# Cross-attention with the values stationary in four column tiles, and the probabilities' sums taken by VectorE and ones

## The chip, the cores and the metric

One core of a Trainium2 chip runs the whole program. The metric is the device time of one execution in microseconds (us); lower is better. Three executions of the kernel before took 1486.96, 1487.69 and 1585.24 us, with 1487.69 us as their median.

## What is computed

The input is x of shape (16, 64, 512) and a context of shape (16, 1601, 256), all in float32. A cross-attention reads the context, a causal self-attention and a mixture of experts follow. The change lies in the cross-attention. Cut to what matters here:

```
q  = ln(x @ Wq + bq)                     # 16 heads of 32
k, v of the first 1585 context rows;  k2, v2 of the last 16 rows ("second" attention)
ctx  = softmax(q k^T / sqrt(32)) v       # over 1585 rows
ctx += softmax(q k2^T / sqrt(32)) v2     # over 16 rows
x = x + ctx @ Wo + bo
```

For each of the 16 batches and 16 heads, 64 queries are weighed over 1585 and over 16 rows. Both softmaxes are normalised after the weighted sum, so the kernel needs, for each query and head, the sum of the exponentials of each attention.

## The kernel before, in words

**Work and its pieces.** The context of a batch is cut into 13 chunks of 128 rows (`CH` = 13); the 13th chunk of two batches shares one tile (49 rows each), and the 16 rows of the second attention lie in that same tile. So two batches, one turn of the outer loop `i`, make 25 projections (`PROJ`) and 26 units of attention (`UNITS`). The units stand in groups (`GROUP`, line 41): five groups of two units and one of three for each batch, 12 groups a turn, 8 turns.

**One group on each engine.** The order is written out by hand in `steps` of each engine.

- TensorE, for each chunk: `keys` (six matmuls of 512 columns into `K_BANK`), `values` (six more into `V_BANK`), `turn` (four transposes of the normalised keys of the group before). Then `weighted` for this group's units and `scores` for the next group's units.
- VectorE, in `chunks`: for each chunk `k_bias` (line 1133, reads PSUM and adds the bias), `k_reduce` (line 1139, sums the squares) and `k_norm` (lines 120, 122, 124 on 16 numbers a row, then line 1148 over 512). The norm of a chunk stands behind the bias of the next one. `queries` (line 1156) copies the next batch's queries in groups 5 and 11; `second_keys` (line 1165) follows groups 1 and 2.
- GpSimd (POOL): `square` (line 1088, the squares of `kc`) and `y_low` (line 1081, the low part of a context chunk).
- ScalarE (ACT): `exps` (line 1004, one of 128x1024 for a unit, into `probs`), `v_evac` (990), `k_evac` (976), `y_high` (963) and `seed` (113 and 115: the start value for the norm).
- SyncE issues the loads.

Every engine works through its own list in order. `keys` of a chunk waits for `k_bias` of the chunk before (semaphore kb), `turn` for `k_norm` of its chunk (km), `weighted` for the exponentials (ex).

**The step that is changed.** In `weighted` (lines 1283 to 1299) the probabilities of a head (128 rows of context by 64 queries) are the stationary operand, and the head's values with a column of ones behind them (`VW1` = 33 columns) move through. Even and odd heads go to PSUM partitions 0 to 63 and 64 to 127, that is two column tiles of 64. The 33rd column of the result is the sum of the probabilities.

```
last = pe.matmul(psum[j * SQ:(j + 1) * SQ, V_BANK if n else O_BANK, p * VW1:(p + 1) * VW1],
                 probs[:, buf(u), place(h) * SQ:(place(h) + 1) * SQ], v, ...)
```

There are 16 such calls for a unit, 32 for the last unit of a batch (which also does the second attention). The trace holds two records for each call with float32 operands. After the last unit ScalarE copies both results to `o_sb` (`o_evac`, 128x264 each), VectorE inverts the sums (line 1209, 16 numbers a row), POOL multiplies and adds (`normalise`, lines 871 and 873, three operations of 128x256), TensorE transposes the result (`turn_ctx`, line 1305), and ScalarE copies it to `ctxT` (`ctx_evac`).

Of the kernel before, what the change touches and what calls it, by code (L numbers as in the profile page):

```python
# [36 lines left out]
VW1 = HD + 1  # L37
# [116 lines left out]
def prepare(nc, io, g, psum):  # L154
    with ExitStack() as ctx:
# [10 lines left out]
        bq = g.o_sb[:].rearrange("p a q n -> p (a q n)")[:, 0:D]  # L166
# [43 lines left out]
        with nc.Block() as block:  # L210
# [102 lines left out]
            def _(pool):  # L313
# [10 lines left out]
                nc.gpsimd.memset(g.v[:], 1.0)  # L324
                nc.gpsimd.memset(g.ctx[:], 0.0)
# [4 lines left out]
                for n, col in enumerate((6, 7, 10, 11)):  # L330
                    nc.gpsimd.tensor_tensor(g.v_last[:, n // 2, n % 2, :, HD], g.v_last[:, n // 2, n % 2, :, HD],
                                            g.cols[:, col:col + 1].to_broadcast([P, H]), ALU.add)
# [413 lines left out]
def cross_attention(nc, io, g, psum):  # L746
# [3 lines left out]
    with ExitStack() as ctx:  # L750
# [4 lines left out]
        kc, o_sb, rinv, od = g.kc, g.o_sb, g.rinv, g.od  # L755
# [8 lines left out]
        probs = sb("probs", [P, 3, H * SQ])  # L764
        select = sb("select", [2, 3, P])
# [45 lines left out]
        def last_unit(u):  # L811

            return u - UNITS + CH if u == TAIL else u - CH if u == UNITS - 1 else u - 2 if column(u) >= 2 else u - 3

# [52 lines left out]

        def normalise(b, wait, engine):

            for n, dst in enumerate((g.ctx, od)):  # L870
                engine.tensor_tensor(dst[:], o_sb[:, n, :, 0:HD], spread(rinv[:, n], HD), ALU.mult).then_inc(s["onp"], 1)
            wait.wait_ge(s["onp"], b * 2 + 2)
            engine.tensor_tensor(g.ctx[:], g.ctx[:], od[:], ALU.add).then_inc(s["on"], 1)

        with nc.Block() as block:
# [69 lines left out]
            def _(act):  # L945
# [5 lines left out]
                act.sem_inc(s["ce"], 1)  # L951
# [55 lines left out]
                def o_evac(b, i, u):  # L1007

                    act.wait_ge(s["pv"], unit(i, u))
                    act.wait_ge(s["on"], b + 1)  # L1010
                    nc.scalar.copy(o_sb[:, 1], psum[:, V_BANK, 0:PAIRS * VW1].rearrange("p (q n) -> p q n", n=VW1))
                    nc.scalar.copy(o_sb[:, 0], psum[:, O_BANK, 0:PAIRS * VW1].rearrange("p (q n) -> p q n", n=VW1))\
                        .then_inc(s["oe"], 1)

                def ctx_evac(b):

                    act.wait_ge(s["ct"], b + 1)
                    nc.scalar.copy(g.ctxT[:, :, :, bass.ds(b * SQ, SQ)],
                                   psum[:, TR_BANK, 0:2 * P].rearrange("p (g j q) -> p g j q", g=2, j=2)).then_inc(s["ce"], 1)
# [22 lines left out]
                def steps(i, room, guarded):  # L1042
                    for group in range(GR):
# [4 lines left out]
                        if group in (1, 7):  # L1048
                            ctx_evac(i * 2 + group // 6)
# [20 lines left out]
            def _(pool):  # L1070
                pool.sem_inc(s["ksq"], PROJ)
                pool.sem_inc(s["ylo"], PROJ + EARLY)
                pool.sem_inc(s["on"], 1)
# [51 lines left out]
            def _(dve):  # L1125
                for stage in ("kb", "krd", "kn1", "kn2", "krs", "km"):
                    dve.sem_inc(s[stage], PROJ)

# [39 lines left out]
                def chunks(i, ns):  # L1168

                    for j, n in enumerate(ns):  # L1170
                        k_bias(i, n)
                        if j:
                            k_norm(i, ns[j - 1])
                        k_reduce(i, n)
                    if ns:
                        k_norm(i, ns[-1])

                def first(guarded):
# [3 lines left out]
                    chunks(0, projections(2, GR))  # L1182
# [20 lines left out]
                def steps(i, room, guarded):  # L1203
                    for group in range(1, GR + 1 if room else GR):
                        if group in (5, 11) and (group == 5 or room):
                            queries(i * 2 + (1 if group == 5 else 2), i, TAIL if group == 5 else UNITS - 1, guarded)
                        if group in (6, 12):
                            dve.wait_ge(s["oe"], i * 2 + (group // 6 + 1))
                            nc.vector.reciprocal(rinv[:], o_sb[:, :, :, HD]).then_inc(s["rc"], 1)
# [1337 lines left out]
```

## Time and profile before

| | us |
|---|---|
| median of three executions | 1487.69 |
| span of the profiled execution, first to last instruction | 1487.2 |
| TensorE matmuls busy | 1399.9 |
| TensorE weight loads busy | 1181.9 |
| VectorE busy | 860.5 |
| ScalarE busy | 778.8 |
| GpSimd busy | 500.8 |

The cross-attention fills the span from about 70 to 1180 us; what comes before prepares the weights and queries, what comes behind it is self-attention and the experts. Times in the trace's views count from the span's start. A timeline row gives start, length, engine, line, operation, result and operands, shapes, and the count of merged instructions; in brackets stands how long the engine sat idle before it, and which instruction ended that.

### The profile page before, as it was taken

To read this page: it belongs to the slowest core of one execution; us is meant where nothing else is said; L and a number is where in the kernel's file an instruction comes from. 1 tells how busy PE (TensorE), PEld (TensorE's weight loads), DVE (VectorE), ACT (ScalarE), POOL (GpSimd) and SP (SyncE) were. 2 spreads that over 40 slices of the span, in tenths; PEclk is the share of its full clock that TensorE was granted. 3 is DMA by queue.
4 is the path that set the end of the run, shared out by engine and by line. 5 is a ranking of instruction groups with operands and counts; after the bars stand their busy time and mean duration, and the time that the engine had idled before them with its cause. 6 is when DMAs were issued, how large, how long until landed. Compare 5 with 4: busy or idle time off the path is not lost. (4 is left out here: it accounts for less than half of the span.)

```text
span 1487.2 us, 41615 instructions
## 1 busy us (share of the span) xinstructions
PE 1399.9 (94%) x15754; PEld 1181.9 (79%) x15754; DVE 860.5 (58%) x2005; ACT 778.8 (52%) x1560; POOL 500.8 (34%) x550
## 2 busy tenths in 40 slices
PE   6789999999999999999999999999999899984796
PEld 3378888888888888888888888888878677764696
DVE  7756555655655565556456555655555356655764
ACT  2345555655555565555555555555555433333653
POOL 3333333333333333333333333333323121111455
PEclk9999999999999999999999999999999999995999
DMA  7042110210111121102101101211010100004886
GB/s 253 19 158 77 31 30 16 91 31 16 62 46 30 30 78 30 30 16 92 30 16 62 48 28 30 78 30 31 17 74 2 60 3 30 30 30 178 220 182 140
DMA packets 38937, 91.24 MB, mean 61 GB/s; under 512 B 8135, under 2 KB 11722, under 8 KB 37258
## 3 DMA queue, kind: packets, MB, share of 16 engines
q1 hardware_dynamic: 31904, 72.38, 14.5%
q0 software_dynamic: 6432, 16.32, 4.8%
q8 instruction: 133, 2.18, 0.6%
q14 instruction: 34, 0.28, 0.1%
q10 hardware_dynamic: 434, 0.08, 0.0%
HBM read 71.93 MB, written 36.01 MB: 73 GB/s over the span
## 5 line engine op out<-in xcount | busy, mean ns | idle before, releaser
L1088 POOL TENSOR_TENSOR ksq<-kc 128x512 f32<-128x512 f32 x200 | 208.4, 1042 | 423.8 <-DVE kc L1133 421.9
L1133 DVE TENSOR_TENSOR kc<-psum,bk_sb 128x512 f32<-128x512 f32 x200 | 138.3, 692 | 235.2 <-PE psum L107 234.7
L990 ACT COPY v_sb<-psum 128x512 f32<-128x512 f32 x192 | 112.7, 587 | 277.2 <-PE psum L107 277.2
L1004 ACT ACTIVATE probs<-psum 128x1024 f32<-128x1024 f32 x208 | 201.0, 1023 | 76.6 <-PE psum L1279 76.5
L1081 POOL TENSOR_TENSOR y_lo<-y_sb,y_hi 128x256 fp32r<-128x256 f32 x190 | 139.8, 736 | 231.4 <-ACT y_hi L963 231.3
L1279 PE MATMUL psum<-qbd,k 64*128 64x128 f32 x3328 | 211.9, 278 | 0.1
L1296 PEld LDWEIGHTS psum<-v_sb,probs 128*64 128x64 f32 x6144 | 187.4, 138 | 18.5 <-issue 18.5
L1139 DVE TENSOR_REDUCE kss<-ksq 128x16 f32<-128x512 f32 x200 | 136.5, 682 | 111.4 <-POOL ksq L1088 111.4
L1296 PE MATMUL psum<-v_sb,probs 128*64 128x33 f32 x6144 | 198.1, 224 | 0.0
L1279 PEld LDWEIGHTS psum<-qbd,k 64*128 64x128 f32 x3328 | 193.3, 188 | 4.5 <-ACT k L976 0.3
L107 PE MATMUL psum<-wk_hi,y_hi 128*128 128x512 f32 x400 | 176.8, 442 | 10.7 <-issue 8.6
L107 PE MATMUL psum<-wv_hi,y_hi 128*128 128x512 f32 x400 | 158.1, 395 | 2.9 <-ACT v_sb L990 2.2
L107 PE MATMUL psum<-wk_hi,y_lo 128*128 128x512 f32 x400 | 158.0, 395 | 0.0
L107 PE MATMUL psum<-wk_lo,y_hi 128*128 128x512 f32 x400 | 157.1, 393 | 0.0
L107 PE MATMUL psum<-wv_hi,y_lo 128*128 128x512 f32 x400 | 156.9, 392 | 0.0
L107 PE MATMUL psum<-wv_lo,y_hi 128*128 128x512 f32 x400 | 156.4, 391 | 0.0
L976 ACT ACTIVATE k<-psum,cols_sb 128x512 f32<-128x512 f32 x192 | 150.6, 784 | 10.6 <-PE psum L88 10.6
L1148 DVE SCALAR_TENSOR_TENSOR kn<-kc,kr 128x512 f32<-128x512 f32 x200 | 141.5, 707 | 7.0
L88 PEld LDWEIGHTS psum<-ident_sb,kn 128*128 128x128 f32 x800 | 98.9, 139 | 26.6 <-issue 0.5
L88 PE MATMUL psum<-ident_sb,kn 128*128 128x128 f32 x800 | 119.8, 272 | 0.0
L122 DVE SCALAR_TENSOR_TENSOR ktmp<-ktmp,kseed 128x16 f32<-128x16 f32 x200 | 115.6, 578 | 6.8
L107 PEld LDWEIGHTS psum<-wk_hi,y_hi 128*128 128x128 f32 x400 | 75.5, 189 | 29.3 <-issue 11.1
(272 smaller groups left out, 1983.9 us busy)
## 6 DMA issues: line engine op xcount, KB each, us to landing
y_sb<-in_y SPq DMA_DIRECT2D x48, 512.0 KB, 3.6
slots_dram<-in_blank SPq DMA_DIRECT2D x9, 2080.0 KB
expert_raw<-in_experts SPq DMA_DIRECT2D x8, 1024.0 KB, 6.9
x_sb<-slots_dram SPq DMA_DIRECT2D x23, 260.0 KB, 3.2
x_sb<-in_x SPq DMA_DIRECT2D x1, 1536.0 KB, 10.7
wq<-in_wq SPq DMA_DIRECT2D x4, 256.0 KB, 4.4
xa_wo<-in_wo SPq DMA_DIRECT2D x1, 1024.0 KB, 12.1
y_tail<-in_y_tail SPq DMA_DIRECT2D x8, 128.0 KB, 21.2
```

What stands on the lines that cost most here:

```text
L88: last = pe.transpose(bank[:, k * P:(k + 1) * P], src[:, k * P:(k + 1) * P], ident)
L107: last = pe.matmul(bank, lhs, rhs, start=(n == 0), stop=(n == len(todo) - 1))
L122: nc.vector.scalar_tensor_tensor(out=tmp, in0=tmp, scalar=-0.5, in1=seed, op0=ALU.mult, op1=ALU.mult).then_inc(second, 1)
L976: last = nc.scalar.activation(k32[:, buf(n)], bank, ACT.Identity, scale=g.cols[:, 2:3], bias=g.cols[:, 3:4])
L1004: nc.scalar.activation(probs[:, buf(u), :], psum[:, bank:bank + 2, :].rearrange("p a n -> p (a n)"), ACT.Exp, scale=SCALE).then_inc(s["ex" ...
L1081: nc.gpsimd.tensor_tensor(g.y_lo[:, buf(n)], src, g.y_hi[:, buf(n)].bitcast(F32), ALU.subtract).then_inc(s["ylo"], 1)
L1088: nc.gpsimd.tensor_tensor(sq[:, buf(n)], kc[:, buf(n)], kc[:, buf(n)], ALU.mult).then_inc(s["ksq"], 1)
L1133: nc.vector.tensor_tensor(kc[:, buf(n)], psum[:, K_BANK, :], g.bk[:], ALU.add).then_inc(s["kb"], 1)
L1139: nc.vector.tensor_reduce(ss[:, buf(n)], head_view(sq[:, buf(n)]), AX_X, ALU.add).then_inc(s["krd"], 1)
L1148: nc.vector.scalar_tensor_tensor(out=head_view(kn[:, buf(n)]), in0=head_view(kc[:, buf(n)]), scalar=HD ** 0.5, in1=spread(kr[:, buf(n)], H ...
L1279: last = pe.matmul(out[n][a], k32[rows, k_buf(u), n, :], g.qbd[rows, n, :], start=not guarded, stop=True, skip_group_check=True)
L1296: last = pe.matmul(psum[j * SQ:(j + 1) * SQ, V_BANK if n else O_BANK, p * VW1:(p + 1) * VW1], probs[:, buf(u), place(h) * SQ:(place(h) + 1 ...
```

## The change

**Weighted sum.** The head's values (128 rows by 32 columns, no column of ones) are now stationary, and the head's probabilities (64 columns) move. Four heads go to four column tiles of 32 (PSUM partitions 0 to 31, 32 to 63, 64 to 95, 96 to 127), so the result comes out with the head's dimensions on the partitions and the queries along the row: 4 x 64 columns for the 16 heads.

**Sums.** VectorE adds up the probabilities of units 0 to 11 of a batch into `total` (128x1024): 11 additions a batch, one for each unit but the first and the last, each placed behind a `k_bias` (`between()` in the diff below does the next addition or, when there is none left, the next reciprocal). At the end of the batch TensorE multiplies `total`, and the last unit's probabilities with two masks of rows, by ones (`counts`: 12 calls of 256 columns, four column tiles), which gives each sum 32 times, on the partitions where the head's results lie.

**Normalising.** `o_sb` holds results and sums, 128x256 of each for each attention. VectorE inverts the sums in four pieces of 128x128 a batch (groups 0, 1 and 2 of the next batch). POOL multiplies twice and adds once (128x256 each, now in group 3 of the next batch), straight into `ctxT`. `turn_ctx` and `ctx_evac` are gone. The last batch's sums are inverted in the self-attention by one VectorE instruction of 128x512. New waits: `exps` waits until the buffer it writes has been added up (pa); the last `counts` waits for the last addition.

```
                 def exps(i, u, j):
                     act.wait_ge(s["pv"], unit(i, last_unit(u)))
+                    if not tail(u):
+                        act.wait_ge(s["pa"], added(i, last_unit(u)))
...
-                        if group in (6, 12):
+                        if group in (3, 9):
                             b = i * 2 + (group // 6 - 1)
-                            pool.wait_ge(s["rc"], b + 1)
-                            pool.wait_ge(s["ct"], b + 1)
+                            pool.wait_ge(s["rc"], b * 4 + 8)
                             normalise(b, pool, nc.gpsimd)
...
+                def add(i, u):
+                    i, u = at(i, u, UNITS)
+                    half = u // CH
+                    dve.wait_ge(s["ex"], unit(i, u))
+                    dve.wait_ge(s["pa"], added(i, u) - 1)
+                    if u - half * CH == 1:
+                        dve.wait_ge(s["pv"], unit(i, half * CH - 1))
+                        nc.vector.tensor_tensor(total[:], probs[:, 0, :], probs[:, 1, :], ALU.add).then_inc(s["pa"], 1)
+                    else:
+                        nc.vector.tensor_tensor(total[:], total[:], probs[:, buf(u), :], ALU.add).then_inc(s["pa"], 1)
+                def invert(b, part):
+                    dve.wait_ge(s["oe"], b + 2)
+                    sums = o_sb[:, part // 2, 1, part % 2 * P:(part % 2 + 1) * P]
+                    nc.vector.reciprocal(sums, sums).then_inc(s["rc"], 1)
...
                     for j, n in enumerate(ns):
                         k_bias(i, n)
+                        between()
                         if j:
                             k_norm(i, ns[j - 1])
                         k_reduce(i, n)
                     if ns:
                         k_norm(i, ns[-1])
+                    while us or parts:
+                        between()
...
-                        for p in range(PAIRS):
-                            for j in range(2):
-                                h = 2 * p + j
+                        bank = V_BANK if n else O_BANK
+                        for k in range(KD):
+                            for r in range(4):
+                                h = k // 2 * 8 + r * 2 + k % 2
...
+                                last = pe.matmul(psum[r * HD:(r + 1) * HD, bank, k * SQ:(k + 1) * SQ], v,
+                                                 probs[:, buf(u), place(h) * SQ:(place(h) + 1) * SQ],
...
+                    if tail(u):
+                        for n, bank in ((1, V_BANK), (0, O_BANK)):
+                            last = counts(bank, g.counted[:, half * 2 + n], probs[:, buf(u), :], n == 1)
+                        pe.wait_ge(s["pa"], added(i, u - 1))
+                        last = counts(O_BANK, g.counted[:, 4], total[:], True)
...
+                def counts(bank, rows, src, stop):
+                    for r in range(4):
+                        last = pe.matmul(psum[r * HD:(r + 1) * HD, bank, KD * SQ:2 * KD * SQ], rows, heads_in(src, r),
+                                         start=False, stop=stop, skip_group_check=True)
```

**What moves on VectorE.** A plain group of two units in the inner loop. Before (`kc` is the biased key chunk, `kss` the sums of squares, `kn` the normalised keys):

```order
L1133 TENSOR_TENSOR kc<-psum,bk_sb 128x512
L1139 TENSOR_REDUCE kss<-ksq 128x16
L1133 TENSOR_TENSOR kc<-psum,bk_sb 128x512
L120 SCALAR_TENSOR_TENSOR ktmp<-kss,kseed 128x16
L122 SCALAR_TENSOR_TENSOR ktmp<-ktmp,kseed 128x16
L124 SCALAR_TENSOR_TENSOR kr<-ktmp,kseed 128x16
L1148 SCALAR_TENSOR_TENSOR kn<-kc,kr 128x512
L1139 TENSOR_REDUCE kss<-ksq 128x16
```

The same stretch of the changed kernel (its lines 1143, 1149, 119 to 123 and 1158 are the ones just named; 1188 is the new addition):

```order
L1143 TENSOR_TENSOR kc<-psum,bk_sb 128x512
L1188 TENSOR_TENSOR total<-total,probs 128x1024
L1149 TENSOR_REDUCE kss<-ksq 128x16
L1143 TENSOR_TENSOR kc<-psum,bk_sb 128x512
L1188 TENSOR_TENSOR total<-total,probs 128x1024
L119 SCALAR_TENSOR_TENSOR ktmp<-kss,kseed 128x16
L121 SCALAR_TENSOR_TENSOR ktmp<-ktmp,kseed 128x16
L123 SCALAR_TENSOR_TENSOR kr<-ktmp,kseed 128x16
L1158 SCALAR_TENSOR_TENSOR kn<-kc,kr 128x512
L1149 TENSOR_REDUCE kss<-ksq 128x16
```

Each bias now has an addition of 128x1024 behind it, ahead of the reduction or the norm.

**What moves on TensorE.** The end of a batch, where its last two units are weighed and the next scores begin. Before:

```order
L1296 MATMUL psum<-v_sb,probs 64x33 x16
L1285 REGISTER_ALU
L1296 MATMUL psum<-v_sb,probs 64x33 x16
L1290 ISA
L1296 MATMUL psum<-v_last,probs 64x33 x32
L1262 ISA
```

And in the changed kernel (`counted` holds the ones and masks):

```order
L1339 MATMUL psum<-probs,v_sb 32x64 x16
L1327 REGISTER_ALU
L1339 MATMUL psum<-probs,v_sb 32x64 x16
L1332 ISA
L1339 MATMUL psum<-probs,v_last 32x64 x32
L1352 MATMUL psum<-probs,counted 32x256 x8
L1345 ISA
L1352 MATMUL psum<-total,counted 32x256 x4
L1304 ISA
```

The number of calls for a unit stays 16 and 32; twelve calls of 256 columns join them at the batch's end, the last four behind a wait for VectorE.

## Rows read from the trace of the kernel before

**Rows 1.** The page: busy time by engine, share of the span, instructions.
```profile
PE 1399.9 (94%) x15754; PEld 1181.9 (79%) x15754; DVE 860.5 (58%) x2005; ACT 778.8 (52%) x1560; POOL 500.8 (34%) x550
```
**Rows 2.** Busy time in one turn of the loop (two batches), from window start to end.
```profile
504.18:640.10 135.92, 135.92 (x1718) 117.87 (x1717) 76.86 (x162) 78.76 (x160) 48.26 (x57) 1.00 0.13 42
```
**Rows 3.** VectorE's waits from 150 to 1080 us: total, times, longest.
```profile
DVE kc L1133 <- PE psum L107: 202.7, 157, 2.6
DVE kss L1139 <- POOL ksq L1088: 95.1, 82, 1.2
DVE ktmp L120 <- ACT kseed L115: 51.7, 83, 0.6
```
**Rows 4.** Timeline of TensorE: two units weighed, their scores, a batch's transpose.
```profile
583.29 0.44 PE L88 MATMUL psum<-ident_sb,ctx_sb 128*128 128x128 f32 x2
...
611.21 2.06 PE L1296 MATMUL psum<-v_sb,probs 128*64 128x33 f32 x64
613.20 2.06 PE L1279 MATMUL psum<-qbd,k 64*128 64x128 f32 x32
```
**Rows 5.** Timeline of TensorE behind the cross-attention and at its end: other tilings, 512 columns.
```profile
1163.48 3.17 PE L1310 MATMUL psum<-xa_wo,ctxT 128*128 128x512 f32 x7
...
1271.78 1.10 PE L1991 MATMUL psum<-sa_kT,sa_qT 64*64 64x128 f32 x32
...
1280.08 1.16 PE L2020 MATMUL psum<-sa_v,sa_pT 128*64 128x66 f32 x32 [0.33 <-ACT sa_pT L1752]
```
**Rows 6.** Timeline of VectorE and POOL through one group of two units.
```profile
606.33 0.69 DVE L1133 TENSOR_TENSOR kc<-psum,bk_sb 128x512 f32<-128x512 f32 x1 [2.05 <-PE psum L107]
...
608.17 0.69 DVE L1139 TENSOR_REDUCE kss<-ksq 128x16 f32<-128x512 f32 x1 [1.15 <-POOL ksq L1088]
...
609.51 0.69 DVE L1133 TENSOR_TENSOR kc<-psum,bk_sb 128x512 f32<-128x512 f32 x1 [0.65 <-PE psum L107]
...
610.12 0.17 DVE L120 SCALAR_TENSOR_TENSOR ktmp<-kss,kseed 128x16 f32<-128x16 f32 x1
...
610.28 1.04 POOL L1088 TENSOR_TENSOR ksq<-kc 128x512 f32<-128x512 f32 x1
610.32 1.03 DVE L122 SCALAR_TENSOR_TENSOR ktmp<-ktmp,kseed 128x16 f32<-128x16 f32 x1
...
611.60 0.69 DVE L1148 SCALAR_TENSOR_TENSOR kn<-kc,kr 128x512 f32<-128x512 f32 x1
...
612.21 0.68 DVE L1139 TENSOR_REDUCE kss<-ksq 128x16 f32<-128x512 f32 x1
612.60 0.73 POOL L1081 TENSOR_TENSOR y_lo<-y_sb,y_hi 128x256 fp32r<-128x256 f32 x1 [1.27 <-ACT y_hi L963]
...
613.51 0.17 DVE L120 SCALAR_TENSOR_TENSOR ktmp<-kss,kseed 128x16 f32<-128x16 f32 x1 [0.62 <-ACT kseed L115]
```
**Rows 7.** Timeline of both where a POOL operation meets one of VectorE.
```profile
93.34 0.69 DVE L1148 SCALAR_TENSOR_TENSOR kn<-kc,kr 128x512 f32<-128x512 f32 x1
...
93.59 1.03 POOL L1081 TENSOR_TENSOR y_lo<-y_sb,y_hi 128x256 fp32r<-128x256 f32 x1 [0.52 <-ACT y_hi L963]
```
**Rows 8.** Groups of VectorE with shapes near the new ones: count, busy us, mean ns.
```profile
L1854 DVE TENSOR_TENSOR sa_s<-sa_s,sa_mx 128x1024 f32<-128x1024 f32 x8 | 9.9, 1234 | 0.3
...
L1209 DVE RECIPROCAL rinv<-o_sb 128x16 f32<-128x16 f32 x15 | 3.8, 254 | 15.7 <-ACT o_sb L1012 15.7
...
L1861 DVE RECIPROCAL sa_ri<-psum 128x8 f32<-128x8 f32 x16 | 2.2, 179 | 2.1 <-PE psum L2020 2.1
```
**Rows 9.** Timeline: queries of the next batch, the three operations that normalise, the handover to self-attention.
```profile
626.85 1.24 DVE L1156 COPY qbd<-q_sb 32x256 f32 x4 [1.38 <-PE psum L1279]
...
638.21 0.62 POOL L871 TENSOR_TENSOR ctx_sb<-o_sb,rinv 128x256 f32<-128x256 f32 x1 [2.89 <-DVE rinv L1209]
...
639.48 0.74 POOL L873 TENSOR_TENSOR ctx_sb<-ctx_sb,od 128x256 f32<-128x256 f32 x1
...
1192.17 0.88 DVE L1841 COPY sa_kT<-psum 32x128 f32<-32x128 f32 x3 [6.78 <-PE psum L96]
```

More of the change, by code:

```diff
@@ L36 @@
 GROUPS = H // 4
-VW1 = HD + 1
 VBUFS = 6
@@ L866, in units, with by_rows, heads_in @@
             return [turn * UNITS + u for u in GROUP[group]]
+        def by_rows(ap):
+            return ap.rearrange("p (g j q) -> p g j q", g=2, j=2)
+        def heads_in(ap, r):
+            return ap.rearrange("p (a g b n) -> p a g b n", a=2, g=2, b=2)[:, r % 2, :, r // 2, :]
         def normalise(b, wait, engine):
[L870 to L873, printed above, removed]
+            for n in range(2):
+                engine.tensor_tensor(o_sb[:, n, 0], o_sb[:, n, 0], o_sb[:, n, 1], ALU.mult).then_inc(s["onp"], 1)
+            wait.wait_ge(s["onp"], b * 2 + 4)
+            engine.tensor_tensor(g.ctxT[:, :, :, bass.ds(b * SQ + SQ, SQ)], by_rows(o_sb[:, 0, 0]), by_rows(o_sb[:, 1, 0]),
+                                 ALU.add).then_inc(s["on"], 1)
         with nc.Block() as block:
@@ L1010, in o_evac @@
                     act.wait_ge(s["on"], b + 1)
[L1011 to L1019, printed above, removed]
+                    for n, bank in ((1, V_BANK), (0, O_BANK)):
+                        last = nc.scalar.copy(o_sb[:, n], psum[:, bank, :].rearrange("p (a n) -> p a n", a=2))
+                    last.then_inc(s["oe"], 1)
                 def first(guarded):
@@ L1176, in chunks, with to_add @@
                         k_norm(i, ns[-1])
+                    while us or parts:
+                        between()
+                def to_add(group, room):
+                    return [u for u in units(group, room) if u % CH not in (0, LAST)]
                 def first(guarded):
@@ L1291, in weighted @@
                     for n in range(2 if tail(u) else 1):
-                        for p in range(PAIRS):
-                            for j in range(2):
-                                h = 2 * p + j
+                        bank = V_BANK if n else O_BANK
+                        for k in range(KD):
+                            for r in range(4):
+                                h = k // 2 * 8 + r * 2 + k % 2
                                 v = g.v_last[:, half, n, h, :] if tail(u) else g.v[:, (u - half) % VBUFS, h, :]
-                                last = pe.matmul(psum[j * SQ:(j + 1) * SQ, V_BANK if n else O_BANK, p * VW1:(p + 1) * VW1],
-                                                 probs[:, buf(u), place(h) * SQ:(place(h) + 1) * SQ], v,
-                                                 start=(p == 0 and (column(u) == 0 or n == 1)), stop=tail(u), skip_group_check=True)
@@ L1349, in steps @@
                             if j < len(turned):
-                                if j == 0 and group in (1, 7):
-                                    pe.wait_ge(s["ce"], i * 2 + (group // 6 + 2))
                                 turn(i, turned[j])
@@ L1798, in _ @@
                     dve.sem_inc(s[stage], 4)
-                nc.vector.reciprocal(g.rinv[:], g.o_sb[:, :, :, HD]).then_inc(s["last_rc"], 1)
+                nc.vector.reciprocal(g.o_sb[:, :, 1], g.o_sb[:, :, 1]).then_inc(s["last_rc"], 1)
                 dve.wait_ge(s["last_rc"], 1)
-                for n, dst in enumerate((g.ctx, g.od)):
-                    nc.vector.tensor_tensor(dst[:], g.o_sb[:, n, :, 0:HD], spread(g.rinv[:, n], HD), ALU.mult).then_inc(s["last_np"], 1)
-                dve.wait_ge(s["last_np"], 2)
-                nc.vector.tensor_tensor(g.ctx[:], g.ctx[:], g.od[:], ALU.add).then_inc(s["last_on"], 1)
+                nc.vector.tensor_tensor(g.o_sb[:, :, 0], g.o_sb[:, :, 0], g.o_sb[:, :, 1], ALU.mult).then_inc(s["last_np"], 1)
+                dve.wait_ge(s["last_np"], 1)
+                first, second = (g.o_sb[:, n, 0].rearrange("p (g j q) -> p g j q", g=2, j=2) for n in range(2))
+                nc.vector.tensor_tensor(g.ctxT[:, :, :, B * SQ:(B + 1) * SQ], first, second, ALU.add).then_inc(s["last_on"], 1)
                 def residual(i, u):
```

72 lines of the change are left out of this document (34 added, 38 removed).

## The prediction

> **What bounds the kernel now.** I read the page first: TensorE is busy 94% of the span, VectorE 58% [rows 1]. Then I took one turn of the loop, two batches, as a window: TensorE is busy all of its 135.92 us, VectorE 76.86, ScalarE 78.76, POOL 48.26 [rows 2]. So a batch costs 67.96 us, and TensorE alone sets that; its granted clock there is 1.00, that is 2.4 GHz. The waits say what the others do: from 150 to 1080 us VectorE waits 202.7 us for TensorE, 95.1 for POOL's squares and 51.7 for ScalarE's seeds [rows 3]. Only the first kind is slack. The other two lie inside VectorE's own chain and stay when it gets more to do. That is the point of this case: work leaves the engine that is the bound and goes to one that looks 43% idle in the loop but is not.
>
> **TensorE, what goes.** Weighing two units is 64 records in 2.06 us, the last one 0.22 long [rows 4]: 1.84 us for the 31 steps between 32 pairs, 0.059 us a pair. A pair is two column tiles at work together. The step for 66 moving columns is (1.16 - 0.22) / 15 = 0.063 us a pair [rows 5], nearly that for 33, so the 64 stationary columns set it, and moving 64 columns instead of 33 costs nothing. Where four tiles of 64 rows by 64 columns are used, 32 records with 128 columns take 1.10 us, the last 0.27 long: 0.83 us for 7 steps, 0.12 us for four [rows 5]. Half the columns should halve that, so I take 0.059 us for four records. A unit is then 8 steps instead of 16 and saves 0.47 us; a batch has 14 such blocks (13 units, the last one double): 6.6 us less.
>
> The new `counts` are 12 calls, 24 records, 6 steps of four. A record of 512 columns takes (3.17 - 0.60) / 6 = 0.43 us [rows 5], one of 256 then 0.215: 1.3 us more. The transpose of the result goes, 0.44 us with its tail [rows 4], some 0.2 in a full queue. Sum for TensorE: 67.96 - 6.6 + 1.3 - 0.2 = 62.5 us a batch. If nothing else bound, 16 batches would save 87 us, and the time would be 1400.
>
> **VectorE, what comes.** Eleven additions of 128x1024 a batch: 1.23 us each by the one row of this shape with two inputs in SBUF [rows 8], 13.6 us. Four reciprocals of 128x128: 16 numbers take 0.254 us, 8 take 0.179 on average [rows 8], 9.4 ns a number, so 1.3 us for 128. A fixed part that differs between PSUM and SBUF makes this rough: by half the slope it would be 0.8, by one and a half of it 1.8. I take 1.2 and keep both ends.
>
> Busy time alone would be 38.4 + 13.6 + 4.8 - 0.3 = 56.5 us a batch, under 62.5. But the engine works in order and shares something with POOL. L122 has the shape of L120, which takes 0.17, but takes 1.03 and ends as POOL's square ends [rows 6]; in the other direction a POOL operation of 0.73 takes 1.03 when it starts under the 0.69 of L1148, and ends 0.59 behind it [rows 7]. A reduction (one input) runs beside POOL's y_lo at its usual 0.68 [rows 6]. So two-input VectorE work and POOL's work exclude each other, and the later one hides about 0.15. The Trainium skill is stricter ("SBUF — State Buffer", section "Who interferes with whom"): the two engines hold the pair of ports exclusively, for the whole instruction, and the other blocks fully. By that rule nothing would be hidden, the 11 squares behind an addition would cost 0.15 us more each, and the time would be some 27 us above the sum below; rows 7 show the 0.15, and I go by them.
>
> The chain of a plain group, from start to start, with the steps of [rows 6]: bias to addition 0.61. The square, released by the bias, comes behind the addition: 1.23 + 0.89, and the reduction starts 0.03 later: 2.15 (today 1.84 from bias to reduction, of which 1.15 idle). Reduction to second bias 0.61, to second addition 0.61. Then addition and second square 1.23 + 0.89, from its end to the next reduction 0.89 as today, and 0.2 for L120: 3.2. Reduction to L120, through ScalarE's seed, 1.30. The last norm 1.23. Sum 9.7 us. Today the same chain has 7.7 and sits inside 10.55.
>
> The six groups of a batch: group 0 has one addition and two reciprocals, 9.9. Groups 1 and 2 have a reciprocal more, 10.8 each. In group 3 POOL normalises first, 2.0 us of which the bias covers 0.6 [rows 9]: 11.1. Group 4: 9.7. Group 5: the queries 1.24 [rows 9], and in every other batch a third chunk of 3.1: 12.4 on average. With 0.2 for `second_keys` that is 64.9, say 65.0 us a batch. One thing is not in it. POOL's y_lo (0.73) starts today only when the norm is over [rows 6]; on a VectorE that runs late its input is ready earlier, and it can slip in between the small steps of the norm: 0 to 0.6 us a group, 0 to 3.6 a batch. I take half: 66.8 us a batch.
>
> That is more than TensorE's 62.5, so VectorE's chain becomes the bound. TensorE can run ahead of it by one bias only (the wait kb), since `keys` uses one bank. The rest of TensorE's gain turns into waiting.
>
> **The rest.** ScalarE's copies of the sums stay of equal size and the copy to `ctxT` goes; ScalarE is 58% busy, nothing. The wait for pa in `exps` asks for an addition two units back, long done. The last `counts` waits for the addition of the unit before, which VectorE passes some 3 us ahead of the weighing; queued behind it are the scores, and they lose nothing as long as VectorE's lag stays under that. The single reciprocal of 128x512 at the handover takes some 4 us more, under an idle stretch of 6.78 us [rows 9].
>
> **Sum.** The profiled execution's span is 1487.2 us, half a microsecond from the median. 16 batches at 66.8 instead of 67.96 save 18.6: 1469 us.
>
> **The rivals.**
> - *TensorE stays the bound.* The additions fall into the holes of VectorE (95.1 us of waiting for POOL [rows 3]) and the square runs beside them. For it speaks the plain busy time of 56.5 against 62.5, against it L122 in [rows 6]. Time 1400, with the doubt in the chain up to 1435.
> - *Four column tiles bring nothing.* No row has four tiles of 128 rows. If only two run together, TensorE takes 67.96 + 1.3 - 0.2 = 69.1 us a batch: 1505 us. The Trainium skill has a rule that points there ("TensorE: Matmul & The Clock Gate", section "Wait — 56ns, not 53.3ns?"): from the start of one matmul to the next there are never less than about 25 ns. The trace does not break it: its densest row has 32 records in 1.10 us [rows 5]. By that rule 448 records a batch, at 29.5 ns today, would save 2 us, TensorE would take 67.1, and the time would be 1473.
> - *VectorE's chain gets longer than a batch is today.* The price of each POOL operation falls on VectorE: y_lo slips in at all 12.5 chunks of a batch, 0.6 each (7.5 us), and the chain is 72.5 with the reciprocals as taken: 1560 us. Half of the y_lo above what I took, and reciprocals of 1.6, give 65 + 3.6 + 1.6 + 0.6 = 70.8: 1533 us, the figure for this case. It decides from the point where the chain passes 67.96 us a batch.
>
> **How the numbers follow.** VectorE's chain as the bound: 0.50, at 1469, own range 1430 to 1515 (65.0 - 1.6 for short reciprocals, 68.6 + 1 for long ones). TensorE as the bound at 1400: 0.23. Four tiles bring nothing, 1505: 0.12. Chain too long, 1533: 0.15. A measurement tells a change from none at about 2%, that is 30 us: below 1458 faster, above 1517 slower. Of the first case 0.14 lies below 1458 and 0.36 within; the second is faster, the third within, the fourth slower but for 0.01. Faster 0.37, within 0.49, slower 0.14. The range leaves out a part of the second and of the fourth case: 1405 to 1520.
>
> **What would show it.** Right: a plain group of 9.7 to 10.3 us; TensorE idle before `keys` with VectorE's bias as releaser, some 4 us a batch; POOL's square starting at the end of an addition or lasting longer by it; 16 calls of `weighted` in half the time of before. Wrong: TensorE busy through the loop in a batch of 62 to 63 us; or 64 records of `weighted` still in 1.9 us; or squares that start 0.1 us behind the bias and last 1.04 while an addition runs. The prediction as a whole falls if a batch takes under 64 or over 70 us.

## The result and the profile after

The changed kernel takes 1518.24 us, median of 4 runs (1515.45 to 1519.64), against 1490.8 for the kernel before on the same chip: ratio 1.0187, 95% interval 1.0154 to 1.0221. It is slower by 1.9%, with an interval that reaches to both sides of the 2% that the prediction asks for. One of the four executions of the kernel before, 1585.24 us, is in the median of 1490.8 and not in the ratio. The forecast was 1469, with a range of 1405 to 1520. So the time lies just inside the range, but on the other side of no change than the likeliest case, whose own range ended at 1515.

The page of the profiled execution after (span 1513.6 us) gives the busy times; the columns are those of [rows 1]:

```profile
PE 1332.0 (88%) x16104; PEld 1081.1 (71%) x16104; DVE 1131.5 (75%) x2227; ACT 776.3 (51%) x1543; POOL 656.9 (43%) x554
```

TensorE is busy 68 us less than before and VectorE 271 more. POOL has 156 us more, with nearly the same instructions. One turn of the loop as a window, with the columns of [rows 2]:

```profile
633.00:772.19 139.19, 127.00 (x1760) 104.75 (x1760) 109.93 (x192) 78.58 (x158) 68.31 (x56) 1.00 0.13 41
```

A batch costs 69.6 us in it instead of 67.96, and 16 times that difference is about the 26.4 us between the two spans. (The seven turns of this trace take 139.2 to 141.3 us, 139.9 on average. The longer ones have a window of group 5, as they are cut below, of up to 14.6 us; e_small_add has such windows too, up to 13.25 us, and what makes them was not looked into.) TensorE, which did not pause once in this window before, now has no record in 12.2 us of it.

Timeline of TensorE after: two units weighed and the start of their scores, then a last unit with its three kinds of tail. They answer to [rows 4]:

```profile
603.95 1.10 PE L1339 MATMUL psum<-probs,v_sb 128*32 128x64 f32 x64
604.99 1.72 PE L1321 MATMUL psum<-qbd,k 64*128 64x128 f32 x26
...
650.05 1.10 PE L1339 MATMUL psum<-probs,v_sb 128*32 128x64 f32 x64
650.97 1.08 PE L1339 MATMUL psum<-probs,v_last 128*32 128x64 f32 x64
651.86 1.05 PE L1352 MATMUL psum<-probs,counted 128*32 128x256 f32 x16
652.72 0.61 PE L1352 MATMUL psum<-total,counted 128*32 128x256 f32 x8
```

Two units take 1.04 us from start to start, 1.99 before: 0.475 us less for each. Of the calls of `counts`, 16 records take 0.86 us, so 0.215 for four; at that rate all 24 take 1.3, and the scores start 1.41 behind the first. TensorE's terms stand as forecast.

Timeline of VectorE and POOL after, through group 2 of a batch and the start of group 3; it answers to [rows 6] and, for POOL's L887 and L889, to [rows 9]:

```profile
610.07 0.63 DVE L1143 TENSOR_TENSOR kc<-psum,bk_sb 128x512 f32<-128x512 f32 x1
610.61 1.21 DVE L1188 TENSOR_TENSOR total<-total,probs 128x1024 f32<-128x1024 f32 x1
612.76 0.69 DVE L1149 TENSOR_REDUCE kss<-ksq 128x16 f32<-128x512 f32 x1 [0.94 <-POOL ksq L1097]
613.36 0.68 DVE L1143 TENSOR_TENSOR kc<-psum,bk_sb 128x512 f32<-128x512 f32 x1
613.96 1.21 DVE L1188 TENSOR_TENSOR total<-total,probs 128x1024 f32<-128x1024 f32 x1
615.09 1.01 DVE L119 SCALAR_TENSOR_TENSOR ktmp<-kss,kseed 128x16 f32<-128x16 f32 x1
616.13 0.65 DVE L121 SCALAR_TENSOR_TENSOR ktmp<-ktmp,kseed 128x16 f32<-128x16 f32 x1
...
620.18 0.94 DVE L1194 RECIPROCAL o_sb<-o_sb 128x128 f32<-128x128 f32 x1
621.04 0.63 DVE L1143 TENSOR_TENSOR kc<-psum,bk_sb 128x512 f32<-128x512 f32 x1
621.58 1.42 DVE L1188 TENSOR_TENSOR total<-total,probs 128x1024 f32<-128x1024 f32 x1
625.57 0.69 DVE L1149 TENSOR_REDUCE kss<-ksq 128x16 f32<-128x512 f32 x1 [2.56 <-POOL ksq L1097]
```
```profile
610.77 1.95 POOL L1097 TENSOR_TENSOR ksq<-kc 128x512 f32<-128x512 f32 x1 [4.78 <-DVE kc L1143]
...
614.12 1.95 POOL L1097 TENSOR_TENSOR ksq<-kc 128x512 f32<-128x512 f32 x1 [0.70 <-DVE kc L1143]
616.03 0.72 POOL L1090 TENSOR_TENSOR y_lo<-y_sb,y_hi 128x256 fp32r<-128x256 f32 x1
621.20 2.40 POOL L887 TENSOR_TENSOR o_sb<-o_sb 128x256 f32<-128x256 f32 x2 [4.44 <-DVE o_sb L1194]
623.80 0.74 POOL L889 TENSOR_TENSOR ctxT<-o_sb 128x256 f32 x1 [0.20 <-POOL o_sb L887]
624.49 1.04 POOL L1097 TENSOR_TENSOR ksq<-kc 128x512 f32<-128x512 f32 x1
```

Both squares of group 2 begin 0.16 us into an addition and last 1.95 us instead of 1.04: each ends 0.9 us behind the addition, and the first reduction starts there. (The square at 624.49, which meets no addition, lasts 1.04.) The first small step of the norm (L119) takes 1.01 us instead of 0.17, until the second square is over. The next one (L121) takes 0.65, because y_lo slipped in. The reciprocal takes 0.94 us, 0.86 from its start to the next.

Waits after, from 150 to 1080 us (waiting engine and line, releaser: total, times, longest):

```profile
DVE kss L1149 <- POOL ksq L1097: 95.8, 80, 2.6
DVE ktmp L119 <- ACT kseed L114: 49.8, 80, 0.6
PE psum L106 <- DVE kc L1143: 43.6, 39, 1.7
DVE kc L1143 <- PE psum L106: 34.2, 28, 2.9
...
PE psum L106 <- ACT probs L1022: 23.1, 14, 2.1
```

VectorE's wait for TensorE fell from 202.7 to 34.2 us, and the other two of [rows 3] stayed. TensorE now waits for VectorE's bias, as forecast, 3.3 us a batch (43.6 us over 13.3 batches, where some 4 were forecast), and 1.65 us in each batch for ScalarE's exponentials, which the prediction did not have. That wait stands at the head of group 5. Here it is on ScalarE, TensorE and VectorE, from the reduction that ScalarE waits for to the first bias of group 0:

```profile
641.35 0.31 ACT L112 ACTIVATE klog<-kss,cols_sb 128x16 f32<-128x16 f32 x1 [2.82 <-DVE kss L1149]
...
644.81 0.50 PE L106 MATMUL psum<-wv_hi,y_hi 128*128 128x512 f32 x1 [2.07 <-ACT probs L1022]
...
656.94 0.69 DVE L1143 TENSOR_TENSOR kc<-psum,bk_sb 128x512 f32<-128x512 f32 x1 [1.70 <-PE psum L106]
```

ScalarE works in order, so its exponentials stand behind the start value for the norm, and that waits for the late reduction. TensorE's values wait for the exponentials; from 644.81 on TensorE does not pause, and the next group's bias waits for it.

Last, the windows from the first bias of one group to the first bias of the next, one turn of after. The groups in order are 4, 5, 0, 1, 2, 3, 4, 5, 0, 1, 2, 3; the queries at the head of group 5 fall into the window of group 4, and the sixth window is the one with a third chunk. The five left out repeat groups 4, 5 and 0 to 2 (11.72, 12.48, 9.65, 10.92, 10.98):

```profile
633.00:644.42 11.42, 8.91 (x134) 7.41 (x134) 9.54 (x19) 7.18 (x14) 5.29 (x4) 1.00 0.16 47
644.42:656.94 12.52, 12.13 (x217) 9.94 (x218) 8.59 (x14) 7.21 (x15) 5.38 (x4) 1.00 0.01 3
656.94:666.61 9.67, 9.67 (x130) 8.17 (x129) 7.91 (x15) 6.11 (x12) 4.48 (x4) 1.00 0.14 39
666.61:677.77 11.16, 11.16 (x138) 9.31 (x136) 9.40 (x18) 6.35 (x13) 5.21 (x4) 1.00 0.04 16
677.77:689.28 11.51, 9.96 (x129) 8.13 (x128) 9.75 (x18) 6.41 (x15) 6.03 (x5) 1.00 0.23 67
689.28:704.48 15.20, 12.73 (x140) 10.21 (x140) 11.67 (x22) 6.42 (x16) 8.52 (x8) 1.00 0.30 120
...
760.23:772.19 11.96, 10.11 (x128) 8.22 (x128) 8.56 (x16) 5.05 (x12) 7.47 (x7) 1.00 0.00 1
```

And two of the same windows of before, groups 5 and 0, where TensorE sets every group but unevenly:

```profile
492.40:504.82 12.42, 12.42 (x193) 10.99 (x192) 6.12 (x13) 6.67 (x14) 5.49 (x7) 1.00 0.01 3
504.82:515.64 10.82, 10.82 (x132) 9.35 (x131) 5.87 (x12) 6.27 (x13) 3.55 (x4) 1.00 0.17 50
```

### The profile page after: what moved, and what is told of

Same layout as the page of the kernel before. It is cut to its first block and busy times, and to the rows that moved or that the text cites. A ratio compares the mean times of both kernels' runs of the same rounds, so it can differ in the third digit from the quotient of the medians.

```text
span 1513.6 us, 42986 instructions
## 1 busy us (share of the span) xinstructions
PE 1332.0 (88%) x16104; PEld 1081.1 (71%) x16104; DVE 1131.5 (75%) x2227; ACT 776.3 (51%) x1543; POOL 656.9 (43%) x554
## 5 line engine op out<-in xcount | busy, mean ns | idle before, releaser
L1097 POOL TENSOR_TENSOR ksq<-kc 128x512 f32<-128x512 f32 x200 | 348.2, 1741 | 446.4 <-DVE kc L1143 445.8
L112 ACT ACTIVATE klog<-kss,cols_sb 128x16 f32<-128x16 f32 x200 | 61.7, 308 | 352.4 <-DVE kss L1149 352.4
L1188 DVE TENSOR_TENSOR total<-total,probs 128x1024 f32<-128x1024 f32 x160 | 196.9, 1231 | 2.8 <-issue 2.0
L1158 DVE SCALAR_TENSOR_TENSOR kn<-kc,kr 128x512 f32<-128x512 f32 x200 | 152.4, 762 | 7.0
L119 DVE SCALAR_TENSOR_TENSOR ktmp<-kss,kseed 128x16 f32<-128x16 f32 x200 | 103.5, 518 | 62.2 <-ACT kseed L114 62.0
```

The costliest lines, as they stand in the source:

```text
L1097: nc.gpsimd.tensor_tensor(sq[:, buf(n)], kc[:, buf(n)], kc[:, buf(n)], ALU.mult).then_inc(s["ksq"], 1)
L1158: nc.vector.scalar_tensor_tensor(out=head_view(kn[:, buf(n)]), in0=head_view(kc[:, buf(n)]), scalar=HD ** 0.5, in1=spread(kr[:, buf(n)], H ...
L1188: nc.vector.tensor_tensor(total[:], total[:], probs[:, buf(u), :], ALU.add).then_inc(s["pa"], 1)
```

## The experiments

All edits are made to the changed kernel, and the diffs are cut to what matters. Times are medians, and ratios are to the kernel before on the same chip; its medians there lie between 1489.0 and 1491.8 us, so a few us between two versions show little.

### Additions of 16 columns (e_small_add)

```diff
+nc.vector.memset(total[:], 0.0)      # once, at the start
...
-    nc.vector.tensor_tensor(total[:], total[:], probs[:, buf(u), :], ALU.add)
+    nc.vector.tensor_tensor(total[:, 0:16], total[:, 0:16], probs[:, buf(u), 0:16], ALU.add)
```

> Leaves out: all but 16 of the 1024 columns of each addition of probabilities (order, waits, counts and reciprocals stay). Theory A (VectorE's in-order chain sets the 69.7 us a batch, through the additions): a batch falls to TensorE's own 62.5 to 64 us, the time to 1400 to 1430. Rival B (TensorE or ScalarE set the batch, by the new counts, the waits for ex and pa, or the shared banks, not VectorE's length): over 1490.

Measured: 1403.93 us, ratio 0.9427 (0.9402 to 0.9452). One turn of it as a window, and the same windows by group as above for its first six (groups 4, 5, 0, 1, 2, 3 with three chunks):

```profile
578.05:588.44 10.39, 10.39 (x145) 8.90 (x144) 7.09 (x18) 7.00 (x14) 3.55 (x4) 1.00 0.18 52
588.44:600.23 11.79, 11.79 (x217) 9.64 (x216) 5.95 (x15) 7.08 (x14) 3.55 (x4) 1.00 0.01 3
600.23:609.90 9.67, 9.67 (x130) 8.17 (x129) 7.01 (x16) 6.01 (x12) 3.55 (x4) 1.00 0.15 41
609.90:619.39 9.49, 9.49 (x129) 8.05 (x128) 6.93 (x16) 6.01 (x12) 3.55 (x4) 1.00 0.05 17
619.39:629.15 9.76, 9.76 (x130) 8.25 (x129) 7.20 (x16) 6.25 (x13) 4.28 (x5) 1.00 0.15 41
629.15:641.76 12.61, 12.46 (x143) 10.17 (x142) 9.04 (x23) 6.99 (x16) 7.08 (x8) 1.00 0.38 140
...
sum 124.89, PE 124.74 PEld 104.69 DVE 83.29 ACT 78.91 POOL 49.18; mean PE 10.39 PEld 8.72 DVE 6.94 ACT 6.58 POOL 4.10
```

This turn takes 124.9 us, so a batch 62.4, with TensorE busy throughout; the seven turns of the trace take 124.9 to 127.4, 62.8 us a batch on average. The additions, with what they hold up, cost the changed kernel 114 us. The reciprocals, the new counts and all new waits are still there, so rival B falls. The rows also give TensorE's own time for each group. It is uneven: 11.8 us in group 5, where the last unit is weighed, and 9.5 to 9.8 in groups 0 to 2.

### Reductions instead of additions (e_reduce_add)

```diff
-    nc.vector.tensor_tensor(total[:], total[:], probs[:, buf(u), :], ALU.add)
+    nc.vector.tensor_reduce(total[:, 0:16], probs[:, buf(u), :].rearrange("p (a n) -> p a n", a=16), AX_X, ALU.add)
```

> Leaves out the sum over units: each addition becomes a reduction of the same 128x1024 probabilities, one input instead of two and as long (1.21 us expected beside 1.23). Theory A1 (an addition costs more than its length, since its two inputs keep POOL's square out): squares start 0.1 us behind the bias and last 1.04 again, some 0.9 us less for each of 11 squares, so the time is 1400 to 1450, bounded by TensorE. Rival A2 (the length of the additions alone makes the chain long, the exclusion costs nothing): 1505 to 1520.

Measured: 1412.88 us, ratio 0.9482 (0.9459 to 0.9505). Its timeline of VectorE and POOL:

```profile
617.78 0.74 POOL L1090 TENSOR_TENSOR y_lo<-y_sb,y_hi 128x256 fp32r<-128x256 f32 x1 [1.02 <-ACT y_hi L979]
...
618.65 1.21 DVE L1190 TENSOR_REDUCE total<-probs 128x16 f32<-128x1024 f32 x1
618.89 1.04 POOL L1097 TENSOR_TENSOR ksq<-kc 128x512 f32<-128x512 f32 x1 [0.38 <-DVE kc L1145]
619.78 0.19 DVE L119 SCALAR_TENSOR_TENSOR ktmp<-kss,kseed 128x16 f32<-128x16 f32 x1
```

VectorE is taken for the same 1.21 us as by an addition, but the square runs under it in its usual 1.04 and L119 is short again. 105 of the 114 us are gone, so rival A2 falls: what lifts VectorE's chain over TensorE's time is that two-input operations and POOL's work exclude each other. (The reduction also writes 16 columns a row and not 1024. The first row above speaks against the writing as what keeps POOL out: y_lo takes its usual 0.74 us beside a bias, 618.04 to 618.73, which reads one input in SBUF and writes 512 columns there.) Here the Trainium skill has the rule in full ("SBUF — State Buffer", section "Who interferes with whom"): a VectorE instruction with two inputs in SBUF contends with a GpSimd instruction that reads SBUF, and a reduction never does on trn2. Both halves of it are seen, in this row and in the 1.95 us of L1097 above.

### The seed behind the next exponentials (e_seed_later)

```diff
 for j, u in enumerate(units(group, room)):
     exps(i, u, j)
+for n in projections(group + 1, room)[-1:]:
+    seed(i, n)
...
-if j < len(project):
+if j < len(project) - 1:
     seed(i, project[j])
...
-seed(0, 3)
```

> On ScalarE the seed of a group's last chunk goes behind the exponentials of the next group instead of ahead of them. Theory C (the loop through ScalarE that the prediction left out: late reduction, seed, exponentials, TensorE's values, VectorE's bias) expects groups 5 and 11 to lose the 2.1 us of TensorE's wait and VectorE some 2.2 us a batch: 1483 (1470 to 1495). Rival (that wait is slack, or VectorE's norm now waits for the later seed as long): 1510 to 1530.

Measured: 1545.94 us, ratio 1.0365 (1.0335 to 1.0394). Theory C's time was wrong, and the rival's figure was too low as well. A line of its waits from 150 to 1080 us, and of its timeline at the end of group 5:

```profile
DVE ktmp L119 <- ACT kseed L114: 102.2, 78, 3.7
```
```profile
528.67 0.18 DVE L119 SCALAR_TENSOR_TENSOR ktmp<-kss,kseed 128x16 f32<-128x16 f32 x1 [2.87 <-ACT kseed L114]
```

TensorE's wait for the exponentials (23.1 us in after) is gone, but a window of group 5 still takes 12.4 us (12.5 in after). That does not show that the wait had cost nothing, for the edit put another in its place: the seed now stands behind exponentials that wait for scores, VectorE waits 102.2 us for seeds instead of 49.8, and the 2.87 us of the second line lie in group 5, whose next bias follows VectorE's own norm and waits for nobody. So the path that theory C names was not tested by itself. Queuing a step that feeds the longest chain behind one that waits for another engine cost 28 us here.

### Additions behind the reductions (e_add_later)

```diff
 k_bias(i, n)
-between()
 if j:
     k_norm(i, ns[j - 1])
 k_reduce(i, n)
+between()
```

> On VectorE each addition goes behind the reduction of its chunk instead of ahead of it (bias, norm of the chunk before, reduction, addition). The square of the first chunk starts at once and the addition of the second chunk covers ScalarE's seed. By the prediction's steps a plain group takes 9.3 instead of 9.7 us; with the 3 squares in 13 that no longer stand under an addition 1 to 4 us a batch less: 1455 to 1500. Rival (the exclusion moves to the norm's last step and to y_lo, nothing is won): 1510 to 1525.

Measured: 1478.02 us, ratio 0.9916 (0.9892 to 0.994). This order alone takes 40 us off and puts the change 0.8% under the kernel before, which is less than the 2%. POOL's squares, from 150 to 1080 us (count, then busy us and mean ns):

```profile
L1097 POOL TENSOR_TENSOR ksq<-kc 128x512 f32<-128x512 f32 x172 | 178.9, 1040 | 380.1 <-DVE kc L1143 375.5
```

In after the mean is 1770 ns. No square meets an addition now, and the addition of the second chunk covers ScalarE's seed (VectorE's wait for it fell from 49.8 to 3.7 us). The exclusion has not gone: the second small step of the norm (L121) now takes 605 ns on average instead of 316, and y_lo 981 instead of 736. A batch takes 67.2 us.

### The same relief in group 3 and in group 5 (e_direct_group3, e_direct_group5)

Units of DIRECT are left out of `to_add`, and ADDS and `added` count only the others:

```diff
+DIRECT = (6, 7)          # e_direct_group5: (10, 11)
...
-return [u for u in units(group, room) if u % CH not in (0, LAST)]
+return [u for u in units(group, room) if u % CH not in (0, LAST) + DIRECT]
...
+if column(u) in DIRECT:
+    last = counts(O_BANK, g.counted[:, 4], probs[:, buf(u), :], False)
```

> Units 6 and 7 of a batch (group 3) are not added on VectorE; TensorE counts them itself, four more calls of counts each. Theory D (a batch costs the sum over its groups of the later of TensorE and VectorE, since only one bias lies between them, not the later of the two sums): group 3 takes 15.2 us with three chunks and 11.96 with two, TensorE's own floor there is 12.6 and 9.7 by the run with small additions; two additions with the squares under them are worth some 2.5 to 3 us there and TensorE pays 0.9, so 2 to 2.7 us a batch are won: 1475 to 1490. Rival E (only the sums over a batch matter): about 3.5 us a batch for two additions with their squares wherever they stand, 1460 to 1470, the same as in group 5.

> The same two additions less on VectorE and two counts more on TensorE, but for units 10 and 11 (group 5). Theory D: group 5 takes 12.5 us, TensorE's own floor there is 11.8, and 0.9 is added to it: nothing is won, 1510 to 1525. Rival E (only the sums over a batch matter): the same time as with units 6 and 7, 1460 to 1490.

Measured: 1482.0 us in group 3, ratio 0.9944 (0.9922 to 0.9966), and 1534.25 in group 5, ratio 1.0304 (1.0269 to 1.034). The work taken off VectorE and put on TensorE is the same, but the results are 52 us apart, which rival E can't give. Group 3 came out as theory D expected: it is VectorE's, and 15.2 and 12.0 become 13.4 and 9.8. Group 5 is TensorE's, so relief of VectorE is worth nothing there, and the new counts are paid in full: in the first batch of a turn its window is 13.4 us instead of 12.5. But 1534.25 is 9 us above theory D's range (1510 to 1525). In the second batch of a turn it takes 13.4 to 15.0 us, more than the counts explain, and why stays open.

### A small y_lo (e_small_ylo)

The chunk that two batches share keeps its full y_lo:

```diff
-nc.gpsimd.tensor_tensor(g.y_lo[:, buf(n)], src, g.y_hi[:, buf(n)].bitcast(F32), ALU.subtract)
+nc.gpsimd.tensor_tensor(g.y_lo[:, buf(n), 0:1, 0:16], src[:, 0:1, 0:16], g.y_hi[:, buf(n), 0:1, 0:16].bitcast(F32), ALU.subtract)
```

> Leaves out all but 16 of the 256 columns of POOL's y_lo, save for the tail chunk (order and waits stay). Theory F (y_lo slips in between the small steps of VectorE's norm and makes them wait, 0.48 us in 5 groups of a batch): 1.5 to 2.4 us a batch less, 1480 to 1495. Rival (that delay is slack, the norm is not on the path): 1510 to 1520.

Measured: 1484.44 us, ratio 0.9955 (0.9939 to 0.9971). The second small step of the norm, in after and in this run (150 to 1080 us):

```profile
L121 DVE SCALAR_TENSOR_TENSOR ktmp<-ktmp,kseed 128x16 f32<-128x16 f32 x166 | 52.5, 316 | 5.7
```
```profile
L121 DVE SCALAR_TENSOR_TENSOR ktmp<-ktmp,kseed 128x16 f32<-128x16 f32 x171 | 34.5, 202 | 5.9
```

A turn takes 135.3 us instead of 139.2, 0.5 less in each window of groups 1 to 4 and nothing in groups 5 and 0. So y_lo, which does no part of the changed work, costs the changed kernel 2.0 us a batch.

### Normalise in group 5 (e_normalise_group5)

```diff
-if group in (3, 9):
+if group in (5, 11):
     pool.wait_ge(s["rc"], b * 4 + 8)
     normalise(b, pool, nc.gpsimd)
```

> POOL's normalise goes from group 3 of the next batch to group 5, nothing else. Theory G (in group 3 it delays the first square and VectorE's reduction behind it, 12.0 us with two chunks against a chain of 10.8 without it; in group 5 TensorE's own 12.4 us cover it): 1.0 to 1.2 us a batch less, 1495 to 1505. Rival (it is the bare number of VectorE's instructions in group 3 that counts, or in group 5 normalise costs as much): 1512 to 1525.

Measured: 1501.26 us, ratio 1.0068 (1.0045 to 1.0091), within what theory G expected. The windows of group 3 fall by more than the 1.2 expected (15.2 to 13.5 and 12.0 to 10.1), but those of group 4 rise by 0.4 to 1.0. Of group 5 those of the first batch of a turn fall from 12.5 to 12.05, and most of the second rise by 1.5 and more, to 14.0 and 15.3. The expected gain came about, but as the sum of gains and losses in several groups.

### Versions that put this together (e_three_edits, e_two_edits, e_three_edits_b, e_four_edits)

All four add behind the reductions (as e_add_later), and ScalarE inverts the sums on its way out of PSUM, so that VectorE has no reciprocals in the loop (the last batch is still inverted at the handover):

```diff
-last = nc.scalar.copy(o_sb[:, n], psum[:, bank, :].rearrange("p (a n) -> p a n", a=2))
+whole = psum[:, bank, :].rearrange("p (a n) -> p a n", a=2)
+nc.scalar.copy(o_sb[:, n, 0], whole[:, 0])
+last = nc.scalar.activation(o_sb[:, n, 1], whole[:, 1], ACT.Ln)
...
+act.wait_ge(s["oe"], b + 2)
+for n in range(2):
+    nc.scalar.activation(o_sb[:, n, 1], o_sb[:, n, 1], ACT.Exp, scale=-1.0).then_inc(s["rc"], 2)
```

e_two_edits is that alone. e_three_edits also counts units 6 and 7 on TensorE, e_three_edits_b units 5 and 7. e_four_edits is e_three_edits with normalise in group 5.

> Three edits together: additions behind the reductions, units 6 and 7 counted on TensorE, and the sums inverted on ScalarE (logarithm on the copy out of PSUM, then an exponential of its negative) instead of by four reciprocals on VectorE. TensorE's floor becomes 63.4 us a batch. By theory D, with additions behind the reductions at 67.2 us a batch today: group 3 falls from 13.4 to 11.7 (1.7), groups 1 and 2 lose a reciprocal of 1.0 each down to the floor (1.0 together), group 0 nothing: 64.5 us a batch, 1435 (1425 to 1450). Rival (ScalarE, 3.5 us shorter on VectorE but with four more steps at the end of a batch, holds back the exponentials of the next group): 1450 to 1475.

> The three edits together without the counting of units 6 and 7 on TensorE: additions behind the reductions, sums inverted on ScalarE. By theory D with the groups of the run of three edits: 1.5 us more in group 3 with three chunks, 0.4 with two, TensorE's 0.9 of counts not seen since VectorE sets those groups: 65.6 us a batch, 1450 (1445 to 1460). Rival E (sums alone): TensorE 62.5, VectorE 3 us more than in the run of three edits: 1465 to 1475.

> The three edits with units 5 and 7 counted on TensorE instead of 6 and 7. Theory D: group 2 stands at 11.3 and 10.8 us against TensorE's 9.8 and 9.6, and gains 1.0 and 0.7; group 3 with three chunks gets an addition back, from 12.5 to 13.2 (TensorE's floor there 12.9): 0.5 us a batch less than the run of three edits, 1435 (1428 to 1442). Rival (with one addition and three chunks group 3 is VectorE's again, 14 us): 1440 to 1448.

> The three edits with units 6 and 7, and normalise in group 5. In the run of three edits normalise slips in between the small steps of VectorE's norm at the end of group 2 (four steps that take 3.2 us instead of 1.2). Theory G: group 2 falls from 11.3 and 10.8 us to 10.1 and 9.8, group 5 rises by at most 0.5: 0.7 us a batch less, 1431 (1425 to 1438). Rival (in group 5 it delays ScalarE's copy of the next sums, which waits for it, and TensorE behind that): 1442 to 1455.

| version | us | ratio to before (95%) |
|---|---|---|
| e_two_edits | 1448.03 | 0.971 (0.967 to 0.975) |
| e_three_edits | 1441.91 | 0.9684 (0.9655 to 0.9713) |
| e_three_edits_b | 1434.83 | 0.9618 (0.958 to 0.9656) |
| e_four_edits | 1456.06 | 0.9764 (0.9725 to 0.9803) |

The first three came within 7 us of the number expected, taken group by group. e_three_edits_b has the lowest time of the four: 3.8% under the kernel before and 83 us under the changed one. One turn of it, as the sum of its windows by group, has TensorE busy for all but 1.5 us:

```profile
sum 128.82, PE 127.34 PEld 104.81 DVE 98.04 ACT 80.44 POOL 54.28; mean PE 10.61 PEld 8.73 DVE 8.17 ACT 6.70 POOL 4.52
```

e_four_edits missed (1425 to 1438 expected, 1442 to 1455 by the rival), by a wait that neither side had named. A line of its waits, 150 to 1080 us:

```profile
PE psum L1360 <- DVE total L1196: 21.8, 14, 1.6
```

Group 2 did fall to 9.8 and 9.6 us. But normalise now runs into the last addition and the norm of group 4 (606.92 to 610.30 in its timeline), and makes the bias and the additions of group 5 late. There the last `counts` waits for the last addition: 1.56 us of TensorE in each batch. In e_three_edits and in e_three_edits_b this wait is 5.7 us in all.

## Why the prediction was wrong

**TensorE's side held.** A saving of 0.47 us for a unit, 1.3 us for the counts and a total of 62.5 us a batch were forecast; 0.475 and 1.3 to 1.4 were measured, and 62.4 to 62.8 a batch once the additions were small. The 1404 us of that run answer to the 1400 of the first rival. The case that four column tiles bring nothing is out. By the rule of "TensorE: Matmul & The Clock Gate" in the Trainium skill (section "Wait — 56ns, not 53.3ns?", 25 ns from start to start at the least) 64 records would take 1.6 us, an estimate from the page's figure. The trace does not agree: they start within 1.04.

**VectorE's steps held.** Group 2 in the timeline takes 10.97 us. Without the reciprocal (0.86) and what y_lo adds to L121 (0.48) that is 9.63, and the plain group was forecast at 9.7. The square behind an addition ends 0.90 us behind it, forecast 0.89. Reciprocals are shorter than taken, 0.86 us instead of 1.2.

**The step that failed is the sum.** "65.0 us a batch" and, after it, "more than TensorE's 62.5, so VectorE's chain becomes the bound" compare two sums over a batch. The same paragraph says that TensorE can run ahead by one bias only, and that works the other way too: where TensorE is the later one in a group, VectorE waits, and can't save the time up for the next group. So a batch costs the sum of the later one in each group, in us (VectorE's column has the prediction's figures, with the queries, half a third chunk and the 0.2 of `second_keys` in the windows where they fall; TensorE's column is measured, since the prediction has no figure by group for it):

| window of group | VectorE's chain as forecast | TensorE's own (e_small_add) | the later | after |
|---|---|---|---|---|
| 4, with the queries | 10.9 | 10.7 | 10.9 | 11.6 |
| 5 | 9.7 | 11.8 | 11.8 | 12.5 |
| 0 | 9.9 | 9.6 | 9.9 | 9.7 |
| 1, 2 | 10.9 each | 9.5, 9.7 | 10.9 each | 11.0, 11.2 |
| 3, mean of two and three chunks | 12.7 | 11.1 | 12.7 | 13.6 |
| batch | 65.0 | 62.4 | 67.1 | 69.6 |

The prediction's chain and TensorE's measured groups, put together this way, give 67.1 + 1.8 for y_lo = 68.9 us a batch, or 1502 us: 33 us of the 49 that were missed. That it adds up group by group is what the two runs with the same relief in different groups show, though theory D's figure for group 5 was 9 us short of the worse of them. (The prediction also set the third chunk in group 5; its products belong to group 5, but its steps are issued in group 3. That moves 1.5 us between rows, not the sum.)

**y_lo** was taken at 1.8 us a batch, half way between bounds. It costs 2.0: 0.48 in each of four groups.

**"The rest"** was taken as nothing, and that was a second mistake: the prediction looked at ScalarE's busy share, and not at what its exponentials stand behind. From the start of TensorE's values at the head of group 5 to the first bias of group 0 it is 12.13 us in after (644.81 to 656.94) and 11.99 in e_small_add (588.24 to 600.23), nearly the same work. But in after the values start 0.39 us behind the first bias of group 5, after 2.07 us of waiting for ScalarE, and in e_small_add 0.20 ahead of it (588.44). These 0.59 us and the 0.14 are the 0.7 by which group 5 stands above TensorE's own 11.8. This is read from the traces; no run takes this wait away and puts nothing in its place.

**Group 3.** Here normalise met an addition: from the start of the addition to the reduction it is 3.99 us (621.58 to 625.57) against 2.15 in the group before, 1.84 more, where the prediction had 1.4. Those 0.44 and y_lo's 0.48 are the 0.9 us of group 3. In group 4 y_lo is 0.48 of the 0.7; the other 0.2 were not traced.

**The rivals.** By its size the result belongs to the fourth case, a batch beyond 67.96 us, with a chance of 0.15: 69.6, where its figure was 70.8. By its cause it belongs to none. That case wanted long reciprocals and a y_lo far above what was taken; the reciprocals were short, y_lo cost 2.0 instead of 1.8, and VectorE's chain alone never was that long, for in group 5 it still waits for TensorE (1.70 us of idle at 656.94). That the time lies inside the stated range is luck: the upper end of 1520 came from the other cases. What a longer batch had in its favour was in the trace: the windows of before take 12.42 us in group 5 and 10.82 in group 0, and the prediction never cut the loop by group for TensorE.

## What to carry to other kernels

- Where two engines hand buffers to each other one at a time, add up the later of the two stage by stage. Sums over a whole loop hide stages where one waits in vain, and relief is worth something only in the stages that the relieved engine sets: the same edit gave -36 us in one group and +16 in another.
- For an engine that is far from busy, look at what its work is queued behind. ScalarE, busy 51% of the span, held TensorE up by 1.65 us a batch, since its exponentials stood behind a step that waited for VectorE.
- An operation put on VectorE with two inputs in SBUF costs its own time and keeps POOL's work out for as long. Put it where nothing waits for POOL (here behind the reduction, over ScalarE's seed: 40 us), and move the small work to an engine that has room for it: with the reciprocals on ScalarE the time fell by another 30 us (1478.0 to 1448.0).

## What was not expected of the hardware

- A reciprocal of 128x128 takes 0.94 us. From 16 and 8 numbers [rows 8] the slope was 9.4 ns a number; the 112 further numbers cost 6.2 ns each ((944 - 254) / 112).
- 64 records of TensorE with 32 stationary and 64 moving columns, in four column tiles of 128 rows, start within 1.04 us: 16 ns apart. Before, 64 records in two column tiles took 1.99 us.
- Two POOL operations under one addition stretch both sides: L887 takes 2.40 us for two (0.74 each in e_reduce_add, which has no additions), and the addition 1.42 instead of 1.21.
